# Attention scores from 96 stacked fp16 rows per head, brought through DRAM one iteration later

## The chip, the cores and the metric

The kernel runs on one core of one Trainium2 chip. The metric is the device time of one execution in microseconds. For scale, three executions of the kernel before took 1156.44, 1158.97 and 1160.72 us.

## What is computed

A Flamingo block: gated cross-attention over a short context, then a gated mixture of experts. There are 2 x 2048 tokens of width 512, 128 context rows, 16 heads of 32, 8 experts of which each token takes 2, and one shared expert.

```python
q = (layernorm(x) @ Wq.T + bq)       # 16 heads of 32
k, v = ctx @ Wk.T + bk, ctx @ Wv.T + bv
att = q @ k.T / sqrt(32)             # per head, [2048, 128]; two masks set entries to -1e9
x = x + tanh(g_xattn) * (softmax(att) @ v)
n = layernorm(x)
p = softmax(n @ router)              # the two largest of 8 weight the experts
x = x + tanh(g_ffn) * (sum of 2 experts(n) + shared expert(n))
```

## The kernel before

The tokens are 32 tiles of 128 rows. There are three passes. **Pass 1** does the attention, the second layernorm and the routing for one tile after the other, and cuts the experts' weights in two fp16 halves beside it. **Pass 2** runs 71 slots of 128 gathered rows through the experts. **Pass 3** does the shared expert and the output. The change is in pass 1; passes 2 and 3 only get other semaphore counts.

Pass 1 is a software pipeline written out by hand. Iteration `it` of every engine's `body` works on several tiles at once: a block that begins with `tile(J, v, lag)` works on tile `it - lag`. Iterations 0 to 11 are written out (`HEAD1`), 12 to 31 are a loop whose trip is two iterations (v = 0 and v = 1), and those from 32 to 39 drain the pipeline (`LAG1` = 8). The order within one iteration is the order of the code on each engine; between engines there are semaphores only. The lags before: 0 first layernorm's statistics; 1 normalised x (ScalarE L584); 2 its transposes (TensorE, L1046), its high fp16 half (ScalarE L556) and low half (VectorE L812), the query product (L1134 to L1136, 48 matmuls) and the move of q to SBUF (ScalarE L607, four instructions); 3 scores (L1099), masked scores with their row maxima (VectorE L782, 16 heads), the shift by the maxima (GpSimd L469) and the exponentials (ScalarE L570, L600); 4 transposes of the probabilities (L1046), their copy (ScalarE L563) and the product with the values (L1119); 5 to 8 the residual, second layernorm (L808 normalises), router and row lists.

The scores of four heads are one fp32 product: 128 rows of q, which hold four heads of 32, against `kbd`, in which each head's keys stand in its own 32 rows and 128 columns and zeros elsewhere.

```python
t.matmul(bank[2 + k % 2][:, :], q_t[u][:, k * P:(k + 1) * P], kbd[:, u, k, :],
         start=True, stop=True).then_inc(s_done, 1)
```

Beside the tiles' work, VectorE searches the weights' peaks in iterations 3 to 11 (L885, two chunks in each of 3 to 7, then one), iteration 11 ends with the spreading of these peaks over the partitions (`spread_peaks`, `scale_of`), and each trip of the loop cuts one chunk: ScalarE writes the high half behind v = 0 (L637), VectorE the low half behind v = 1 (L915). Iterations 32 to 34 cut three more (ScalarE L630, VectorE L907). SyncE issues the tile's loads and stores from one queue, in the order of its `body`.

## Time and profile before

| | us |
|---|---|
| three executions, median | 1158.97 (1156.44 to 1160.72) |
| the profiled execution | 1153.63, of which the span 1151.9 |
| pass 1, to the last cast of its row list | 523 |
| plan and first gathers, until TensorE is in full work | to about 560 |
| passes 2 and 3 | from there to 1152 |
| mean granted TensorE clock | 0.957 of 2.4 GHz |

Two executions of one kernel differ by up to 4 us here. The timelines count from the first instruction. A busy time counts overlapping instructions of an engine once; a matmul's own duration (0.22 us for one of 128 columns) includes its way through the array, so that what one adds to the engine's time is the distance between starts.

### The profile page before, as it was taken

Reading aid. Unit: us, or ns where it says so; the run is one execution under the profiler, and the core shown is the slowest. Engines: PE = TensorE matmul, PEld = TensorE weight load, DVE = VectorE, ACT = ScalarE, POOL = GpSimd, SP = SyncE. Lnnn points to the kernel's source line nnn. Section 1 sums busy time; section 2 is a strip of 40 time slices with the busy share of each in tenths; the row PEclk is TensorE's granted clock in tenths of the full one; section 3 lists DMA queues with packets and bytes.
Section 4 is the critical chain, followed back from the end, with each engine's and each line's share of the span. In section 5 each row is a group of like instructions: output and inputs, shape, how many; then the busy total and the mean of one; then the engine's idle time right before and its main releaser. Section 6 shows DMA issues by size and latency. Waiting matters only on the chain.

```text
span 1151.9 us, 26618 instructions
## 1 busy us (share of the span) xinstructions
PE 1044.5 (91%) x7344; PEld 670.6 (58%) x7345; DVE 823.4 (71%) x2938; ACT 530.7 (46%) x1041; POOL 444.0 (39%) x654
## 2 busy tenths in 40 slices
PE   5899969999999999851899999999999999999996
PEld 4677758777777777640455555555554444444443
DVE  5999868888888888673576666666665566666666
ACT  2455536666666666540444444444443223232322
POOL 4345547666666666442211221221110423232322
PEclk9999989999999999865899999999999999999999
DMA  7564753334433332432233333333332645454444
GB/s 284 184 237 168 165 118 95 95 95 93 109 80 108 104 91 90 101 93 73 83 111 118 109 119 118 109 118 119 109 119 71 184 148 166 152 169 150 168 150 128
DMA packets 76731, 146.96 MB, mean 128 GB/s; under 512 B 20912, under 2 KB 23088, under 8 KB 73872
## 3 DMA queue, kind: packets, MB, share of 16 engines
q1 hardware_dynamic: 46512, 66.01, 20.9%
q10 hardware_dynamic: 17280, 44.83, 10.3%
q0 software_dynamic: 12896, 35.58, 10.0%
q8 instruction: 22, 0.36, 0.2%
q14 instruction: 21, 0.17, 0.2%
HBM read 94.04 MB, written 52.35 MB: 127 GB/s over the span
## 4 chain that ended last, share of the span: by engine, by line
PE 58%; issue 11%; DVE 11%; POOL 8%; DMA 5%; ACT 3%; POOLq 1%; SPq 0%; another core or an unknown queue 0%; DVEq 0%; ACTq 0%
PE bank L1054 15%; PE bank L1055 15%; PE bank L1056 15%; PE bank L1046 8%; DVE arena L782 3%; PE bank L1099 3%; DMA arena<-in_x 3%; POOL arena L469 3%; PE bank L1119 2%; POOL token_of_row L505 2%; DVE arena L871 1%; DVE peak L885 1%; POOL arena L476 1%; ACT arena L607 1%; DMA token_of_row<-arena 1%
## 5 line engine op out<-in xcount | busy, mean ns | idle before, releaser
L1054 PE MATMUL bank<-weights,arena 128*128 (+1 forms) x682 | 260.0, 381 | 2.1 <-ACT arena L649 1.9
L1055 PE MATMUL bank<-weights,arena 128*128 (+1 forms) x682 | 260.0, 381 | 0.0
L1056 PE MATMUL bank<-weights,arena 128*128 (+1 forms) x682 | 259.7, 381 | 0.0
L1046 PE MATMUL bank<-ident,arena 128*128 128x128 f32 (+1 forms) x1592 | 188.3, 266 | 52.9 <-DMA arena<-normed_rows,arena 26.3
L1046 PEld LDWEIGHTS bank<-ident,arena 128*128 128x128 f32 (+1 forms) x1592 | 160.7, 132 | 99.9 <-issue 69.3
L516 POOL DMA_INDIRECT arena<-normed_rows,arena x71 | 67.1, 946 | 255.1 <-PE bank L1046 238.4
L1099 PE MATMUL bank<-arena 128*128 128x512 f32 x256 | 138.8, 646 | 11.0 <-DVE arena L782 8.9
L1119 PEld LDWEIGHTS bank<-arena 128*128 128x128 f32 x1024 | 128.3, 194 | 34.9 <-issue 28.0
L469 POOL TENSOR_TENSOR arena<-arena 128x512 f32<-128x512 f32 x96 | 101.3, 1055 | 83.0 <-DVE arena L782 81.9
L526 POOL DMA_INDIRECT arena<-expert_rows,arena x64 | 62.8, 982 | 173.8 <-DVE arena L1006 156.1
L1119 PE MATMUL bank<-arena 128*128 128x33 f32 x1024 | 125.3, 273 | 3.3 <-ACT arena L563 3.3
L782 DVE CUSTOM_DVE_ANT_0 arena<-bank,arena 128x128 f32<-128x128 f32 x512 | 116.8, 283 | 15.0 <-PE bank L1099 11.2
L570 ACT ACTIVATE arena<-arena 128x512 f32<-128x512 f32 x96 | 60.6, 631 | 125.5 <-POOL arena L469 125.2
L1056 PEld LDWEIGHTS bank<-weights,arena 128*128 128x128 f16 x682 | 66.9, 98 | 81.0 <-issue 1.3
L1054 PEld LDWEIGHTS bank<-weights,arena 128*128 128x128 f16 x682 | 66.9, 98 | 72.2 <-issue 4.4
L1055 PEld LDWEIGHTS bank<-weights,arena 128*128 128x128 f16 x682 | 66.8, 98 | 69.9 <-issue 1.1
L978 DVE TENSOR_SCALAR arena<-bank,arena,w_back 128x512 f32<-128x512 f32 x71 | 57.5, 810 | 55.5 <-PE bank L1056 55.4
L1134 PE MATMUL bank<-arena 128*128 128x128 f16 x512 | 87.4, 219 | 1.4 <-DVE arena L812 1.4
L1136 PE MATMUL bank<-arena 128*128 128x128 f16 x512 | 87.4, 219 | 0.0
L1135 PE MATMUL bank<-arena 128*128 128x128 f16 x512 | 87.4, 219 | 0.0
L505 POOL DMA_INDIRECT token_of_row<-arena x64 | 66.3, 1035 | 38.1 <-POOL arena L502 17.3
L658 ACT ACTIVATE arena<-arena 128x256 f16<-128x256 f32 x71 | 36.0, 508 | 91.3 <-DVE arena L990 91.3
(175 smaller groups left out, 1895.8 us busy)
## 6 DMA issues: line engine op xcount, KB each, us to landing
expert_rows<-arena ACTq DMA_DIRECT2D x71, 256.0 KB, 2.1
arena<-in_x SPq DMA_DIRECT2D x64, 256.0 KB, 2.8
weights<-in_w_gu ACTq DMA_DIRECT2D x8, 1024.0 KB, 4.9
x_rows<-arena SPq DMA_DIRECT2D x32, 256.0 KB
normed_rows<-arena SPq DMA_DIRECT2D x32, 256.0 KB
normed_transposed<-arena SPq DMA_DIRECT2D x32, 256.0 KB
arena<-normed_transposed SPq DMA_DIRECT2D x32, 256.0 KB, 3.2
arena<-x_rows SPq DMA_DIRECT2D x32, 256.0 KB, 3.5
```

What stands on the lines that cost most here:

```text
L469: g.tensor_tensor(sc, sc, mx, ALU.subtract).then_inc(shift_done, 1)
L505: g.indirect_dma_start(list_dram, bass.IndirectOffsetOnAxis(ap=row_i[u][:, k:k + 1], axis=0), tok_i[u], None).then_inc(rows_out[u], 16)
L782: last = d.tensor_tensor_reduce(score[u][:, hh * T:(hh + 1) * T], bank[2 + k % 2][:, h * T:(h + 1) * T], mask_bias[u], 1.0, LOWEST, ALU.ad ...
L1046: last = t.transpose(dst[:, c * P:(c + 1) * P], src[:, c * P:(c + 1) * P], (ident16 if src.dtype == F16 else ident)[:, :])
L1054: t.matmul(dst, hi[:, rows], w_hi(c), start=(c == 0), stop=False)
L1055: t.matmul(dst, hi[:, rows], w_lo(c), start=False, stop=False)
L1056: last = t.matmul(dst, lo[:, rows], w_hi(c), start=False, stop=(c == chunks - 1))
L1099: t.matmul(bank[2 + k % 2][:, :], q_t[u][:, k * P:(k + 1) * P], kbd[:, u, k, :], start=True, stop=True).then_inc(s_done, 1)
L1119: last = t.matmul(bank[6 + half][:, at:at + D + 1], probs_t[k % 2][:, h * P:(h + 1) * P], vaug[:, u, k * HG + h, :], start=True, stop=True)
L1134: t.matmul(dst, wq[:, 0, at:at + P], x_hi[:, xs], start=(ci == 0), stop=False)
L1135: t.matmul(dst, wq[:, 0, at:at + P], x_lo[:, xs], start=False, stop=False)
L1136: last = t.matmul(dst, wq[:, 1, at:at + P], x_hi[:, xs], start=False, stop=(ci == EC - 1))
```

## The change

- **Scores.** q and k are written as fp16 halves, high and low. For each head 96 rows are stacked by `stack`: part 0 (the high half), part 1 (the low half) and part 0 of its 32 rows, of q and of k alike. One fp16 matmul of 96 x 128 by 96 x 128 per head gives what four heads together had from one fp32 matmul of 512 columns: 16 matmuls for four.
- **The way of q.** ScalarE writes the high half of q (one instruction instead of four), VectorE the low half (new, first in its next iteration), SyncE stores both to DRAM (256 KB) and, when that has landed, loads the stack with three DMAs of 128 KB. Scores and all behind them are therefore one iteration later: lag 4 and so on, `LAG1` = 9, one iteration more in all.
- **The way of k**, once, in iteration 2: peak, scale, halves, a store to DRAM and three loads; the memset of `kbd` goes away and the sixteen small moves of k become four of all partitions.
- **Bias of q**: four more fp16 matmuls of 64 rows per tile, instead of the bias operand of L607. The exponentials scale by `score_scale`.
- **Order.** The transposes of x stand behind the first value product on TensorE. ScalarE's high half of x stands behind the first two probability copies and ahead of the exponentials. VectorE's low half of x stands behind the second group of maxima. SyncE issues q's store, x, the residual's x and the stack first, then the stores.
- **Semaphores** of passes 2 and 3 are merged; the spreading of the peaks uses bank 4 in place of bank 0.

```diff
+SMALL = 2.0 ** -20
+BIAS_PART = 32.0
+Q_DOWN = 2.0 ** -19
+STACK = 3 * D
...
+    q_dram = nc.dram_tensor("query_halves", [B, 2, P, E], F16).ap()
+    k_dram = nc.dram_tensor("key_halves", [2, P, EC * B * T], F16).ap()
...
-        kbd = carve(B * EC * HG * T).rearrange("p (b c n) -> p b c n", b=B, c=EC)
+        k_stack = carve(B * H * T // 2).bitcast(F16)
...
-        q_t = [carve(E) for _ in range(2)]
+        q_halves = carve(E).bitcast(F16)
+        q_stack = [carve(H * T // 2).bitcast(F16) for _ in range(2)]
...
-        LAG1, LAG2, LAG3, SPAN2 = 8, 4, 4, 4
+        LAG1, LAG2, LAG3, SPAN2 = 9, 4, 4, 4
...
-                n, j, u = tile(J, v, 6)
+                n, j, u = tile(J, v, 3)
+                if live(n, NT):
+                    hold(sp, sp_passed, (q_ready, n + 1))
+                    sp.dma_start(q_dram[u].rearrange("a p n -> p a n"), q_halves.rearrange("p (a n) -> p a n", a=2)).then_inc(q_out[u], 16)
+                n, j, u = tile(J, v, 0)
+                if live(n, NT):
+                    need(sp, xn_ready, n - 1)
+                    sp.dma_start(x_in[u], x_tiles[bass.ds(j + u * HALF, 1)].rearrange("a p d -> (a p) d")).then_inc(x_here[u], 16)
+                n, j, u = tile(J, v, 5)
+                if live(n, NT):
+                    need(sp, x1_ready, n - 1)
+                    sp.dma_start(x_res[u], x_tiles[bass.ds(j + u * HALF, 1)].rearrange("a p d -> (a p) d")).then_inc(res_here[u], 16)
+                n, j, u = tile(J, v, 3)
+                if live(n, NT):
+                    hold(sp, sp_passed, (q_out[u], 16 * (j + 1)))
+                    hold(sp, sp_passed, (s_done, group(n - 2, EC - 1)))
+                    stack(q_stack[u], q_dram[u], q_stacked[u])
+                n, j, u = tile(J, v, 7)
...
+                n, j, u = tile(J, v, 8)
...
-                n, j, u = tile(J, v, 0)
-                if live(n, NT):
-                    need(sp, xn_ready, n - 1)
-                    sp.dma_start(x_in[u], x_tiles[bass.ds(j + u * HALF, 1)].rearrange("a p d -> (a p) d")).then_inc(x_here[u], 16)
+                n, j, u = tile(J, v, 1)
+                if live(n, NT):
...
-                n, j, u = tile(J, v, 4)
-                if live(n, NT):
-                    need(sp, x1_ready, n - 1)
-                    sp.dma_start(x_res[u], x_tiles[bass.ds(j + u * HALF, 1)].rearrange("a p d -> (a p) d")).then_inc(res_here[u], 16)
+            def stack(dst, src, done):
+
+                for at, part in enumerate((0, 1, 0)):
+                    sp.dma_start(dst[at * D:(at + 1) * D, :].rearrange("d (h n) -> d h n", h=HG),
+                                 src[part].rearrange("(h d) n -> d h n", h=HG)).then_inc(done, 16)
 
+                if it == 2:
+                    sp.wait_ge(k_lo_set, 1)
+                    sp.dma_start(k_dram.rearrange("a p n -> p a n"), k_halves.rearrange("p (a n) -> p a n", a=2)).then_inc(k_out, 16)
+                    sp.wait_ge(k_out, 16)
+                    stack(k_stack, k_dram, k_stacked)
...
@@ ScalarE @@
             def body(J, v):
-                n, j, u = tile(J, v, 2)
-                if live(n, NT):
-                    act.wait_ge(xt_done, n + 1)
-                    need(act, q_done, n)
-                    a.activation(x_hi, bank[0][:, :], ACT.Copy, scale=X_SCALE).then_inc(hi_ready, 1)
-
                 def take_probs(k):
-                    n, j, u = tile(J, v, 4)
+                    n, j, u = tile(J, v, 5)
                     if live(n, NT):
...
                 take_probs(0)
                 take_probs(1)
+                n, j, u = tile(J, v, 2)
+                if live(n, NT):
+                    act.wait_ge(xt_done, n + 1)
+                    need(act, q_done, n)
+                    a.activation(x_hi, bank[0][:, :], ACT.Copy, scale=X_SCALE).then_inc(hi_ready, 1)
                 exponent(0)
...
-                        last = a.activation(sc, sc, ACT.Exp, bias=peaks_neg[:, h - H + HG:h - H + HG + 1])
+                        last = a.activation(sc, sc, ACT.Exp, scale=score_scale[:, :], bias=peaks_neg[:, h - H + HG:h - H + HG + 1])
...
                     act.wait_ge(q_done, n + 1)
-                    need(act, s_done, group(n - 2, EC - 1))
-                    for c in range(EC):
-                        last = a.activation(q_t[u][:, c * P:(c + 1) * P], bank[0][:, c * P:(c + 1) * P], ACT.Identity,
-                                            scale=w_back[:, 0:1], bias=bq_s[:, c:c + 1])
-                    last.then_inc(q_ready, 1)
+                    hold(act, act_passed, (q_out[(v - 3) % 2], 16 * (j + u)))
+                    a.activation(q_halves[:, 0:E], bank[0][:, :], ACT.Copy, scale=Q_DOWN).then_inc(q_hi_ready, 1)
 
             def beside(it):
+                if it == 2:
+                    act.wait_ge(scale_set, 3)
+                    a.activation(k_halves[:, 0:EC * B * T], k_full, ACT.Copy, scale=w_scale[:, 5:6]).then_inc(k_hi_set, 1)
...
@@ VectorE @@
-                dve.wait_ge(kv_set, 1)
+                dve.wait_ge(kv_mm, 1)
                 for c in range(EC):
-                    dve.wait_ge(kv_mm, 1)
-                    for h in range(HG):
-                        rows = slice(h * D, (h + 1) * D)
-                        last = d.tensor_scalar(kbd[rows, :, c, h * T:(h + 1) * T], bank[K_BANK + c][rows, 0:B * T].rearrange("p (b t) -> p b t", b=B),
-                                               bk_s[rows, c:c + 1], float(D) ** -0.5, ALU.add, ALU.mult)
-                last.then_inc(kv_set, 1)
+                    last = d.tensor_scalar(k_full[:, c * B * T:(c + 1) * B * T], bank[K_BANK + c][:, 0:B * T], bk_s[:, c:c + 1],
+                                           float(D) ** -0.5, ALU.add, ALU.mult)
+                link(last)
+                d.tensor_reduce(peak[:, 20:21], k_full, AX.X, ALU.max, apply_absolute_value=True).then_inc(peak_set, 1)
+                spread_peaks(1, 2)
+                scale_of(5, 1, 20, SMALL)
+                d.tensor_scalar(score_scale[:, :], w_back[:, 0:1], w_back[:, 5:6], 1.0 / Q_DOWN, ALU.mult, ALU.mult).then_inc(kv_set, 1)
+                dve.wait_ge(k_hi_set, 1)
+                d.scalar_tensor_tensor(k_halves[:, EC * B * T:], k_full, w_scale[:, 5:6], k_halves[:, 0:EC * B * T],
+                                       ALU.mult, ALU.subtract).then_inc(k_lo_set, 1)
...
+                n7, j7, u7 = tile(J, v, 8)
+                n8, j8, u8 = tile(J, v, 9)
+                n, j, u = tile(J, v, 3)
+                if live(n, NT):
+                    dve.wait_ge(q_hi_ready, n + 1)
+                    d.scalar_tensor_tensor(q_halves[:, E:2 * E], bank[0][:, :], Q_DOWN, q_halves[:, 0:E], ALU.mult, ALU.subtract).then_inc(q_ready, 1)
...
-                n, j, u = tile(J, v, 2)
-                if live(n, NT):
-                    dve.wait_ge(hi_ready, n + 1)
-                    d.scalar_tensor_tensor(x_lo, bank[0][:, :], X_SCALE, x_hi, ALU.mult, ALU.subtract).then_inc(lo_ready, 1)
...
                 maxima(1)
-                normalise(1, 5)
+                n, j, u = tile(J, v, 2)
+                if live(n, NT):
+                    dve.wait_ge(hi_ready, n + 1)
+                    d.scalar_tensor_tensor(x_lo, bank[0][:, :], X_SCALE, x_hi, ALU.mult, ALU.subtract).then_inc(lo_ready, 1)
...
@@ TensorE @@
-                    n, j, u = tile(J, v, 3)
+                    n, j, u = tile(J, v, 4)
                     if live(n, NT):
-                        pe.wait_ge(q_ready, n + 1)
+                        pe.wait_ge(q_stacked[u], 16 * PARTS * (j + 1))
+                        pe.wait_ge(k_stacked, 16 * PARTS)
                         need(pe, max_done, group(n, k - 2))
-                        if it_is_first(n, k):
-                            pe.wait_ge(kv_set, 2)
-                        t.matmul(bank[2 + k % 2][:, :], q_t[u][:, k * P:(k + 1) * P], kbd[:, u, k, :],
-                                 start=True, stop=True).then_inc(s_done, 1)
+                        for h in range(HG):
+                            q_at, k_at = (h * EC + k) * P, ((h * EC + k) * B + u) * T
+                            last = t.matmul(bank[2 + k % 2][:, h * T:(h + 1) * T], q_stack[u][0:STACK, q_at:q_at + P],
+                                            k_stack[0:STACK, k_at:k_at + T], start=True, stop=True)
+                        last.then_inc(s_done, 1)
...
-                                last = t.matmul(dst, wq[:, 1, at:at + P], x_hi[:, xs], start=False, stop=(ci == EC - 1))
+                                t.matmul(dst, wq[:, 1, at:at + P], x_hi[:, xs], start=False, stop=False)
+                            last = t.matmul(dst, bq_half[:, co * P:(co + 1) * P], bias_row[:, :], start=False, stop=True)
...
                 mix_values(0)
+                n, j, u = tile(J, v, 2)
+                if live(n, NT):
+                    pe.wait_ge(xn_ready, n + 1)
+                    need(pe, q_ready, n)
+                    transposes(bank[0], xn[u], EC).then_inc(xt_done, 1)
                 scores(2)
...
             def beside(it):
                 if it == 2:
+                    turn_peaks(1, 2)
                     values()
                 if it == SPREAD_IT:
-                    pe.wait_ge(q_ready, it - 1)
-                    turn_peaks(0, 2)
-                    pe.wait_ge(scale_set, 4)
+                    turn_peaks(4, 3)
+                    pe.wait_ge(scale_set, 5)
```

## Rows read from the trace of the kernel before

**Rows 1.** The page: busy time by engine, and two groups of instructions.
```profile
PE 1044.5 (91%) x7344; PEld 670.6 (58%) x7345; DVE 823.4 (71%) x2938; ACT 530.7 (46%) x1041; POOL 444.0 (39%) x654
...
L1119 PE MATMUL bank<-arena 128*128 128x33 f32 x1024 | 125.3, 273 | 3.3 <-ACT arena L563 3.3
L782 DVE CUSTOM_DVE_ANT_0 arena<-bank,arena 128x128 f32<-128x128 f32 x512 | 116.8, 283 | 15.0 <-PE bank L1099 11.2
```
**Rows 2.** Windows: stretch, length, busy PE, PEld, DVE, ACT, POOL, clock, DMA, GB/s.
```profile
60.00:120.00 60.00, 55.99 (x535) 46.76 (x535) 57.78 (x253) 37.21 (x84) 32.27 (x51) 1.00 0.55 186
...
300.00:360.00 60.00, 56.65 (x540) 47.34 (x536) 49.94 (x272) 39.73 (x89) 39.21 (x56) 0.94 0.32 92
```
**Rows 3.** Timeline of VectorE over two iterations: start, duration, instruction, idle time before.
```profile
317.53 0.54 DVE L808 TENSOR_SCALAR arena<-arena 128x512 f32<-128x512 f32 x1
320.85 0.69 DVE L812 SCALAR_TENSOR_TENSOR arena<-bank,arena 128x512 f16<-128x512 f32 x1 [2.78 <-ACT arena L556]
322.42 0.29 DVE L782 CUSTOM_DVE_ANT_0 arena<-bank,arena 128x128 f32<-128x128 f32 x1 [0.88 <-PE bank L1099]
...
346.24 0.54 DVE L808 TENSOR_SCALAR arena<-arena 128x512 f32<-128x512 f32 x1
```
**Rows 4.** Timeline of ScalarE between the same two iterations.
```profile
316.94 1.50 ACT L607 ACTIVATE arena<-bank,bq_s,w_back 128x128 f32<-128x128 f32 x4
318.30 2.02 ACT L637 ACTIVATE weights<-weights,w_scale  x1
320.20 0.62 ACT L556 ACTIVATE arena<-bank 128x512 f16<-128x512 f32 x1
```
**Rows 5.** Windows of TensorE alone around that place: stretch, length, busy, clock, DMA.
```profile
316.00:320.00 4.00, 2.49 (x32) 0.95 0.87 309
320.00:324.00 4.00, 4.00 (x14) 0.62 0.06 17
```
**Rows 6.** Timeline of VectorE: first and last start of twenty loop iterations, and the peaks.
```profile
155.16 0.69 DVE L871 BATCH_NORM_STATS2 arena<-arena 128x6 f32<-128x512 f32 x1 [4.73 <-DMA arena<-in_x]
...
163.28 0.55 DVE L808 TENSOR_SCALAR arena<-arena 128x512 f32<-128x512 f32 x1 [0.45 <-DVE w_scale L741]
...
448.74 0.54 DVE L808 TENSOR_SCALAR arena<-arena 128x512 f32<-128x512 f32 x1
```
**Rows 7.** The chain that ended last, in order of time: start, its length, what.
```profile
328.30 0.06 PE bank L1134
...
334.44 1.72 PE bank L1099 x4
```
**Rows 8.** Timeline of VectorE at the start.
```profile
26.28 7.91 DVE L762 TENSOR_SCALAR arena<-bank,bk_s 32x256 f32<-32x256 f32 x16
...
35.42 0.68 DVE L812 SCALAR_TENSOR_TENSOR arena<-bank,arena 128x512 f16<-128x512 f32 x1
...
41.65 4.45 DVE L885 TENSOR_REDUCE peak<-weights 128x1 f32<-128x2048 f32 x2
```
**Rows 9.** Timeline of TensorE at the start.
```profile
25.56 7.08 PE L1081 MATMUL bank<-arena 128*128 128x512 f32 x16
```
**Rows 10.** DMA issues before 180 us: x loads, count, KB, us to landing.
```profile
arena<-in_x SPq DMA_DIRECT2D x24, 256.0 KB, 7.3
```
**Rows 11.** The same from 180 to 450 us.
```profile
arena<-in_x SPq DMA_DIRECT2D x37, 256.0 KB, 2.7
```
**Rows 12.** The queue of SyncE: start and duration of one issue.
```profile
49.85 0.43 SPq L384 DMA_DIRECT2D arena<-in_x  x1
```
**Rows 13.** Timeline of VectorE in the iterations behind the loop.
```profile
463.36 2.35 DVE L907 SCALAR_TENSOR_TENSOR weights<-weights,w_scale 128x2048 f16<-128x2048 f32 x1 [3.55 <-ACT weights L630]
...
479.74 2.35 DVE L907 SCALAR_TENSOR_TENSOR weights<-weights,w_scale 128x2048 f16<-128x2048 f32 x1 [4.07 <-ACT weights L630]
482.01 0.54 DVE L808 TENSOR_SCALAR arena<-arena 128x512 f32<-128x512 f32 x1
...
495.27 2.35 DVE L907 SCALAR_TENSOR_TENSOR weights<-weights,w_scale 128x2048 f16<-128x2048 f32 x1 [2.16 <-ACT weights L630]
```

237 lines of the change are left out of this document (128 added, 109 removed).

## The prediction

> **What bounds the kernel now.** I read the page's busy times first: TensorE is at work for 91% of the span, VectorE for 71% [rows 1]. That is a mean over passes with different limits, so I went to the windows by stage. The change is in pass 1. There both engines are close to full: between 60 and 120 us VectorE has 57.78 of 60 us, in the loop (300 to 360 us) TensorE 56.65 and VectorE 49.94 [rows 2]. Work taken from TensorE is therefore worth no more than the room VectorE leaves.
>
> That room is read from VectorE's timeline over one trip of the loop, two iterations [rows 3]. From one L808 (317.53) to the next but one (346.24) are 28.71 us. In it VectorE waits twice for long: 2.78 us at L812 for ScalarE's high half of x, 0.88 us at L782 for the first scores. The rest, 28.71 - 2.78 - 0.88 = 25.05 us, is work, with short gaps of 0.2 us between dependent instructions. ScalarE's timeline shows where the 2.78 us come from [rows 4]: four moves of q (1.50 us) and the split of a weight chunk (L637, 2.02 us) stand ahead of L556 in its queue. TensorE is held by the same moves of q, since its transposes of x wait for the bank: in this window it is busy for 2.49 of 4 us, and in the next 4 us its granted clock is 0.62 of 2.4 GHz, thus a good part of it at 1.2 GHz [rows 5]. The mean over the loop: iterations 12 to 31 take 448.74 - 163.28 = 285.46 us [rows 6], 28.55 us a trip.
>
> **TensorE's part.** Two fp32 score products take 1.72 us of the chain, four 3.44; an fp16 matmul of 128 columns starts 0.06 us after the one before it [rows 7]. The new sixteen are 16 x 0.06 = 0.96 us, the four of the bias 0.24. TensorE loses 3.44 - 1.20 = 2.2 us of work in each of 32 iterations, 72 us in all. From 56.65 / 60 x 14.27 = 13.5 us an iteration it falls to 11.2, and no longer bounds. If it alone counted, the kernel would be 72 us faster; that is the far end on that side.
>
> **VectorE's part in the loop.** It gains one instruction per tile, the low half of q. Its form (fp16 from PSUM, 128 x 512, one fp16 operand) is L812's, 0.69 us [rows 3], 1.38 us a trip. The two long waits should go: the moves of q become one instruction (L556's form, 0.62 us in place of 1.50 [rows 4]), x's low half now stands behind two groups of maxima, and scores come from a tile that was ready an iteration ago. Work alone gives 25.05 + 1.38 = 26.4 us a trip. Some wait stays. In the v = 1 iteration ScalarE comes out of the chunk's split 2.02 us late, and then has two copies of probabilities ahead of x's high half, which in turn needs TensorE's first value product and the transposes. Starting from the low half of q at 0, ScalarE is free at about 1.4, has copied by 2.4, TensorE's value product and transposes end at 3.3 (125.3 / 1024 x 8 = 1.0 for eight products [rows 1] is in it), the high half at 4.0; VectorE reaches the low half at 3.5 (0.69 + 0.54, eight maxima at 116.8 / 512 = 0.23 [rows 1], 0.5 of small ones). So about 0.4 us. And TensorE now idles more in each trip, so more of its stretches will be at 1.2 GHz; one of them in front of that same path costs VectorE about 1 us. I take 0.5 us a trip for it. Sum 26.4 + 0.4 + 0.5 = 27.3, against 28.55: -1.25 us a trip, -12.5 us in ten. Bounds: 26.4 (-21.5) and 28.9 (+3.5, where TensorE is late at each step, see the second rival).
>
> GpSimd isn't next: it is busy for 39.21 of 60 us [rows 2], and gets no work in the loop. ScalarE loses 0.88 us an iteration and isn't next either.
>
> **SyncE's queue in the loop.** It issues ten DMAs an iteration in place of five or six, 0.43 us each [rows 12], 4.3 us of 13.7. It waits for the low half of q, stores it, issues two x loads while the store is under way, waits for the store, and issues three loads. By the x loads' 2.7 us to landing [rows 11] the stack is there 0.7 + 0.43 + 2.7 + 1.3 + 2.7 = 7.8 us after VectorE's iteration begins, and TensorE asks for it after a whole iteration, 13.7 us. The x load of the same iteration is issued at about 1.6 and needed near its end. The stores of the residual and of the normalised rows now stand behind the wait for the stack, with some 4 us to spare. I cost all this at nothing; if the cover were gone, each us of delay would be one us an iteration. The 640 KB of new traffic raises a DMA share of 0.32 [rows 2] by the ratio of bytes (five transfers of 256 KB before) to about 0.5: the engines are not full.
>
> The Trainium skill speaks of this way too. DMA: Bandwidth & Descriptors, section Anatomy of one DMA, gives each DMA a fixed cost of some 2 us that hardly depends on its size and comes mostly from confirming the write. By it the two dependent steps would cost 4 us beside their bytes, which is still hidden in the loop; the landing times of [rows 11] already hold it, and no run here shows the part alone.
>
> **The start.** The sixteen small moves of k (L762) take 7.91 us, 0.49 each; four of all partitions, at the same 0.49, end at 26.3 + 2.0 = 28.3 [rows 8]. Then come a search of 1024 columns (half of one of the two L885, 1.1), the spreading and one scale (3.6; with two scales it took some 4.4, what is left of the 8.1 us from 155.16 to 163.28 [rows 6] behind 1.4 of the iteration's rest and a search of 2.2), ScalarE's half (half of L637, 1.0) and VectorE's (half of L907's 2.35 [rows 13], 1.2): 35.2. The store and the loads follow, and only behind them SyncE's x of tile 3, which VectorE needs to end iteration 3. Two landings in a row, at 2.7 to 7.3 us each [rows 10, 11], and 1.7 us of issues: x is there at 42 to 51.5, I take 47.5. With 0.9 us of statistics and the two searches (4.45) iteration 4 begins at 52.8. TensorE's values product (7.08 us, [rows 9]) moves behind the peaks' spreading and ends at 39, under the same cover. Its first scores need the stack of tile 0, another two landings: +1.5, at 54.3. Before, the first scoring iteration began at 35.42 [rows 8]. So 18.9 us are lost, but iterations 3 to 11 scored nine tiles there and score eight now. Those nine took 163.28 - 35.42 = 127.9 us, of which 4.4 spreading and 4.7 a wait for x, so 13.2 each. The start costs 18.9 - 13.2 + 8 x 0.69 = +11.2; taken off are the waits for ScalarE and the first scores there (about 4.8) and one search and the lighter mix of what drops out (some 3). Rounded, +3.5 us at the loop's first iteration, with 0 and +10 as its ends, from the two landing times.
>
> **The end.** One iteration with scores more. Such a one, without the layernorm of x, took 495.27 - 2.16 - 482.01 = 11.1 us [rows 13], at a slow TensorE; with the short scores about 10.5. In the three before, VectorE waits for ScalarE's chunk (3.55, 4.07, 2.16 us [rows 13]). The shorter move of q takes 0.88 off two of them, faster scores about 1.6 over all, the low halves of q give 2.1 back: -1.3. The end costs +9, from +6 to +12. Pass 2 and 3: nothing, their waits are the same ones under other counts.
>
> **Sum.** +3.5 - 12.5 + 9 = 0. The profiled execution took 1153.63, so it would be again; it was 5.3 us under the median of the runs. I forecast the median: 1159 us.
>
> **The rivals.** *VectorE runs without waits.* For it: in the iterations between 60 and 120 us it is at 96% [rows 2] although TensorE is then nearly full too. Then the trip is 26.4, the start +1 and the end +9: -21.5 + 10 = -11.5, 1147 us. Faster. Chance 0.34.
>
> *TensorE's clock.* This ends on the other side. TensorE's work a trip falls to 22.4 us, of which the stretch at the low clock cost 0.38 x 4 = 1.5, so to 20.9 at 2.4 GHz, in 27: near a quarter of the time idle, in pieces of 1 to 2 us, where one piece of 1.5 us was enough for a stretch at 1.2 GHz [rows 5]. If half of its time is granted at 1.2 GHz, the work takes 20.9 / 0.75 = 27.9 us, longer than VectorE's 27.3, and two engines that hand over to each other several times a trip then take more than either: 28.9. That gives +3.5 in the loop, and with a slower start (+5) and end (+10) +18, 1177 us. It decides from about two low stretches a trip on, where there was one. Against it: TensorE waits for VectorE at most places, so much of a low stretch is cover. Chance 0.16. The Trainium skill has the rule, in TensorE: Matmul & The Clock Gate, section A second HAM failure mode: short idles between groups of matmuls are enough to let the clock swing. By [rows 5] the trace agrees for the one place there is.
>
> *The way through DRAM is late where the weights are loading.* There x loads take 7.3 us to land [rows 10]; the stack would need 0.7 + 0.43 + 7.3 + 1.3 + 7.3 = 17 us against iterations of 13.2. With 3 to 4 us of wait in half of eight iterations, +14, and the kernel is at 1172 us. It decides where a landing takes over 5.4 us. Against it: a chunk's load is over well before the next, so few stacks meet one. Chance 0.12.
>
> The forecast itself, within about 6 us of no change, has 0.38.
>
> **How the numbers follow.** 0.5% (6 us) is about what a measurement of this kernel can tell from no change. Faster 0.34 is the first rival, slower 0.28 the two others, 0.38 the forecast. The likeliest case alone covers 1153 to 1165. The range reaches to the first rival and 3 us beyond it, and to the late way through DRAM: 1144 to 1175.
>
> **What would show it.** L1099 at 16 matmuls an iteration, about 0.9 us. VectorE at over 90% of the loop with no wait of 2.8 us at x's low half; a trip of 27.3 us, the loop from about 167 to 440 us; the low half of q at 0.69. No wait of TensorE for the stack after 180 us. The pass 1 end at 523 give or take 6. The prediction is wrong if the trip is under 26.5 or over 28.5, if TensorE waits for the stack in the loop, or if the first scores come before 48 or after 60 us.

## The result and the profile after

The changed kernel takes 1190.32 us (median of 4 runs, 1176.83 to 1199.91) against 1157.70 us for the kernel before (4 runs). Two of the four runs, the profiled one of 1199.91 us among them, showed a lower granted clock and over 1.5% more time than the fastest, so the ratio is that of the other two, 1.0195 with a 95% interval of 1.0125 to 1.0265. In a second comparison it took 1181.35 us (6 runs) against 1154.45 (17 runs): ratio 1.0249, interval 1.0208 to 1.0291. It is 2.5% slower. The forecast was 1159 us and no change, and the range ended at 1175. Executions also scatter more than the 4 us of the first three: those 17 of the kernel before lie between 1149.46 and 1162.29 us, the six of the changed kernel between 1177.53 and 1191.09.

What follows reads the profile of the second comparison, an execution of 1180.61 us. Its page, busy times by engine and the group of the new score products:

```profile
PE 1047.2 (89%) x7731; PEld 708.2 (60%) x7732; DVE 839.3 (71%) x2970; ACT 528.5 (45%) x946; POOL 443.0 (38%) x658
...
L1155 PE MATMUL bank<-arena 96*128 96x128 f16 x512 | 52.4, 244 | 28.7 <-DMA arena<-query_halves 16.8
```

TensorE is as busy as before [rows 1] although its long products are gone, and it sat idle for 16.8 us ahead of the new ones, waiting for q's stack. Windows by stage, columns as in [rows 2]:

```profile
60.00:120.00 60.00, 54.66 (x552) 49.36 (x551) 55.84 (x198) 34.71 (x66) 25.64 (x44) 0.86 0.64 216
120.00:180.00 60.00, 41.26 (x427) 37.85 (x424) 42.20 (x211) 25.15 (x52) 26.29 (x41) 0.79 0.70 185
180.00:240.00 60.00, 56.19 (x532) 52.61 (x531) 45.84 (x252) 37.59 (x70) 33.16 (x48) 0.78 0.71 134
240.00:300.00 60.00, 55.39 (x548) 50.92 (x547) 51.07 (x264) 37.38 (x71) 38.28 (x56) 0.82 0.73 120
300.00:360.00 60.00, 54.77 (x600) 50.08 (x599) 54.23 (x266) 38.43 (x73) 40.51 (x58) 0.91 0.71 149
```

The kernel before, in two of these stretches:

```profile
180.00:240.00 60.00, 56.29 (x521) 45.67 (x519) 51.05 (x277) 39.61 (x88) 41.58 (x59) 0.97 0.32 90
240.00:300.00 60.00, 56.73 (x546) 47.78 (x546) 50.52 (x271) 40.40 (x88) 40.83 (x57) 0.97 0.41 97
```

Two columns differ. The granted clock between 180 and 300 us is 0.78 and 0.82, so a large part of that stretch ran at 1.2 GHz. The DMA share is 0.7, where it was 0.32 to 0.41 and where I had worked out "about 0.5".

To see where the time goes I take one mark in each iteration that no kernel here moves, the start of VectorE's statistics of x (L871 before, L935 after). For tiles 11 and 31, and the last low half of pass 1, VectorE's timeline after:

```profile
170.74 0.68 DVE L935 BATCH_NORM_STATS2 arena<-arena 128x6 f32<-128x512 f32 x1
...
464.70 0.68 DVE L935 BATCH_NORM_STATS2 arena<-arena 128x6 f32<-128x512 f32 x1
...
538.16 0.69 DVE L932 SCALAR_TENSOR_TENSOR arena<-bank,arena 128x512 f16<-128x512 f32 x1 [0.74 <-ACT arena L641]
```

Before, the mark of tile 11 is at 155.16 [rows 6] and the last low half at 511.5: pass 1 ends 26.7 us later, and the spans differ by 26.9 (1178.8 and 1151.9). Passes 2 and 3 cost what they did. The stages of one profiled execution of each kernel, in us between these marks ("way" is q's store to DRAM and the three loads of the stack):

| kernel | mark 3 | 3 to 9 | 9 to 11 | 11 to 21 | 21 to 31 | to the end of pass 1 |
|---|---|---|---|---|---|---|
| before | 40.8 | 80.3 | 34.0 | 146.7 | 143.1 | 66.6 |
| changed | 49.5 | 80.6 | 40.6 | 155.8 | 138.1 | 73.5 |
| changed, without the way | 50.5 | 76.8 | 26.4 | 147.9 | 136.1 | 73.5 |
| changed, way in the loop alone | 50.2 | 80.5 | 28.5 | 153.0 | 146.3 | 73.9 |
| changed, way unread, SyncE still waits | 49.4 | 81.6 | 42.9 | 157.5 | 138.0 | 79.1 |
| changed, reload at 32 | 49.9 | 80.0 | 29.2 | 156.4 | 137.8 | 85.1 |
| changed, reload spread | 49.7 | 88.4 | 29.3 | 158.2 | 142.5 | 73.9 |
| no way, scores four times | 50.2 | 83.7 | 30.3 | 166.9 | 145.1 | 81.1 |
| before, x moved | 40.5 | 82.2 | 31.3 | 148.8 | 137.7 | 66.1 |

Each row is one execution, and a stage scatters by several us. The kernel with the spread reload has the code of the changed kernel up to mark 9 and yet shows 88.4 for 80.6. The medians below decide. What is sharp is iteration 11. VectorE and TensorE in the changed kernel, waits between 140 and 182 us (total, times, longest):

```profile
PE bank L1155 <- DMA arena<-query_halves: 14.2, 1, 14.2
DVE arena L872 <- DMA normed_rows<-arena: 13.8, 1, 13.8
```

SyncE's queue shows why. L383 is q's store, L416 the stack, issued once the store has landed, L404 the store of the normalised rows. Iteration 11, then one late in the loop:

```profile
147.66 0.38 SPq L383 DMA_DIRECT2D query_halves<-arena  x1
148.08 0.51 SPq L387 DMA_DIRECT2D arena<-in_x  x1
148.64 0.47 SPq L391 DMA_DIRECT2D arena<-in_x  x1
162.64 1.27 SPq L416 DMA_DIRECT2D arena<-query_halves  x3
163.96 0.43 SPq L400 DMA_DIRECT2D x_rows<-arena  x1
164.43 0.43 SPq L404 DMA_DIRECT2D normed_rows<-arena  x1
...
427.12 0.38 SPq L383 DMA_DIRECT2D query_halves<-arena  x1
...
429.55 1.28 SPq L416 DMA_DIRECT2D arena<-query_halves  x3
```

Over pass 1 (40 to 540 us) TensorE waits 16.8 us for the stack, of which 0.3 after 180 us, and VectorE 19.1 us in three waits for the store of the normalised rows. Before there was no wait for that store.

From the store's issue to the stack's the forecast had 3.1 us (0.43 + 2.7). Late in the loop it is 2.4. In iteration 11 it is 15.0, in the one before 6.9, and twice in the first half of the loop 7.9 and 9.3. In iterations 10 and 11 ScalarE's queue is loading 3 MB of w_down again. The Trainium skill has a reason for so late a landing, in DMA: Bandwidth & Descriptors, section Queues, rings and completion order: the increment that reports a transfer lands only after every earlier write of the same DMA engine, from whichever queue. Nothing here shows that step by itself, but the trace does not speak against it.

### The profile page after: what moved, and what is told of

Read it like the earlier page. It is cut to its first block, busy times and chain, and to the rows that moved or that the text cites. A ratio compares the mean times of both kernels' runs of the same rounds, so it can differ in the third digit from the quotient of the medians.

```text
span 1198.1 us, 28092 instructions
## 1 busy us (share of the span) xinstructions
PE 1071.2 (89%) x7731; PEld 728.5 (61%) x7732; DVE 840.3 (70%) x2970; ACT 528.9 (44%) x946; POOL 442.0 (37%) x658
## 4 chain that ended last, share of the span: by engine, by line
PE 65%; DVE 12%; issue 9%; DMA 7%; POOL 3%; ACT 1%; SPq 1%; POOLq 1%; DVEq 0%; another core or an unknown queue 0%; ACTq 0%
PE bank L1111 14%; PE bank L1113 14%; PE bank L1112 14%; PE bank L1103 10%; PE bank L1176 6%; DVE arena L842 4%; PE bank L1155 2%; PE bank L1192 2%; DMA arena<-in_x 1%; DMA normed_rows<-arena 1%; PE bank L1194 1%; PE bank L1193 1%; DVE peak L949 1%; DMA token_of_row<-arena 1%; DVE arena L935 1%
## 5 line engine op out<-in xcount | busy, mean ns | idle before, releaser
L1103 PE MATMUL bank<-ident,arena 128*128 128x128 f32 (+1 forms) x1592 | 220.7, 288 | 52.5 <-DMA arena<-normed_rows,arena 27.2
L1103 PEld LDWEIGHTS bank<-ident,arena 128*128 128x128 f32 (+1 forms) x1592 | 181.9, 146 | 83.1 <-issue 49.6
L1176 PE MATMUL bank<-arena 128*128 128x33 f32 x1024 | 154.1, 305 | 3.8 <-ACT arena L606 2.1
L1176 PEld LDWEIGHTS bank<-arena 128*128 128x128 f32 x1024 | 146.3, 223 | 8.4 <-ACT arena L606 3.2
L842 DVE CUSTOM_DVE_ANT_0 arena<-bank,arena 128x128 f32<-128x128 f32 x512 | 116.7, 282 | 20.1 <-PE bank L1155 14.2
L1113 PEld LDWEIGHTS bank<-weights,arena 128*128 128x128 f16 x682 | 67.0, 98 | 81.1 <-issue 1.8
L1192 PE MATMUL bank<-arena 128*128 128x128 f16 x512 | 105.0, 237 | 3.1 <-DVE arena L889 3.1
L1193 PE MATMUL bank<-arena 128*128 128x128 f16 x512 | 103.9, 235 | 0.0
L1194 PE MATMUL bank<-arena 128*128 128x128 f16 x512 | 103.4, 234 | 0.4 <-issue 0.4
L613 ACT ACTIVATE arena<-arena,score_scale 128x512 f32<-128x512 f32 x96 | 69.0, 719 | 51.2 <-POOL arena L508 49.9
L606 ACT ACTIVATE arena<-bank 128x512 f32<-128x512 f32 x128 | 70.3, 589 | 45.5 <-PE bank L1103 45.2
L1155 PE MATMUL bank<-arena 96*128 96x128 f16 x512 | 54.9, 252 | 30.2 <-DMA arena<-query_halves 16.8
```

Source lines behind the costliest of these rows:

```text
L606: a.activation(probs_t[k % 2], bank[4 + k % 2][:, :], ACT.Copy).then_inc(pt_ready, 1)
L842: last = d.tensor_tensor_reduce(score[u][:, hh * T:(hh + 1) * T], bank[2 + k % 2][:, h * T:(h + 1) * T], mask_bias[u], 1.0, LOWEST, ALU.ad ...
L1103: last = t.transpose(dst[:, c * P:(c + 1) * P], src[:, c * P:(c + 1) * P], (ident16 if src.dtype == F16 else ident)[:, :])
L1113: last = t.matmul(dst, lo[:, rows], w_hi(c), start=False, stop=(c == chunks - 1))
L1155: last = t.matmul(bank[2 + k % 2][:, h * T:(h + 1) * T], q_stack[u][0:STACK, q_at:q_at + P], k_stack[0:STACK, k_at:k_at + T], start=True, ...
L1176: last = t.matmul(bank[6 + half][:, at:at + D + 1], probs_t[k % 2][:, h * P:(h + 1) * P], vaug[:, u, k * HG + h, :], start=True, stop=True)
```

## The experiments

Five theories. **A**: the stores, put behind the stack's wait in SyncE's queue, are late. **B**: q's way itself, by its traffic. **C**: TensorE with less to do runs at the lower clock, which eats what was saved. **S**: the reload of w_down in iterations 10 and 11 holds q's way up. **W**, against B taken as the bytes: the waits for q's way. All ratios are to the kernel before on the same chip, with their 95% intervals.

**The changed kernel again**, unchanged: the reference for the others.

> The changed kernel once more, unchanged: a second profile to read the others against. Expected by every theory: 1177 to 1192 us, ratio to before 1.015 to 1.025, and again one long wait of VectorE for the store of normed_rows in iteration 11 (14.2 us in the first profile), if that wait belongs to the order of the queue and isn't an accident of one execution (then it is gone, and the time is near 1177).

1181.35 us, 1.0249 (1.0208 to 1.0291). The long wait is there again (13.8 us): it belongs to the kernel.

**The stores ahead of the wait** (A).

```diff
+ (x1, xn2, x2t stores of tiles n-7, n-8)     # behind q's store
  (two loads of x)
  hold(q_out); hold(s_done); stack(...)
- (x1, xn2, x2t stores of tiles n-7, n-8)
```

> Changed kernel with SyncE's three stores (x1, xn2, x2t) issued ahead of the two waits for q's store and the stack, right behind q's own store. Theory A (the loss is what stands behind the stack's wait in SyncE's queue, above all the 14.2 us wait of iteration 11): VectorE no longer waits for normed_rows, 14 to 20 us less than the changed kernel, 1162 to 1172. Theory B (it is the 128 KB stores and 1 KB packets of q's way that slow every transfer): at most 3 to 5 us less. Theory C (TensorE's clock falls because it has less to do): no change, or up to 3 us less.

1181.41 us, 1.0236 (1.0199 to 1.0273): nothing. VectorE's wait for the rows is gone, but between 118 and 182 us TensorE waits 15.7 us for the stack and VectorE 7.6 for x. A falls as the explanation of the 24 us: which transfer is late depends on the order, that one is late doesn't. The two waits of SyncE, for the low half of q and for q's store, still stand in its queue here.

**Without q's way** (B).

```diff
-if live(n, NT):                # q's store, and the stack
+if isinstance(n, int) and 0 <= n < 2:
...
-pe.wait_ge(q_stacked[u], 16 * PARTS * (j + 1))
+pe.wait_ge(q_stacked[u], 16 * PARTS)
```

> Changed kernel in which q goes through DRAM for tiles 0 and 1 only; all later scores are taken from the stacks of those two, so the fresh q is left out and the DMA way (one store, three loads a tile) with it; all products and evictions stand. Theory A: the same gain as from stores first, 14 to 20 us less than the changed kernel. Theory B: 25 to 35 us less, 1150 to 1160, DMA share of the loop back to about 0.35 and packets of 2048 bytes back to about 114 ns. Theory C: no more than 5 us less, and the granted clock between 180 and 300 us stays at 0.80 or below (0.80 and 0.78 in the changed kernel; 0.88 later in its loop).

1157.53 us (12 runs), 1.0036 (1.0011 to 1.0062). B holds in that the way as a whole costs 1.0249 / 1.0036 = 1.021, some 24 us. Two things go with it at once, though: its traffic, and the two waits of SyncE ahead of x and of the stores. The DMA share does not fall to the 0.35 expected, and the clock of 180 to 300 us is still low in part:

```profile
180.00:240.00 60.00, 56.66 (x560) 51.36 (x560) 52.45 (x269) 37.42 (x71) 39.47 (x56) 0.83 0.51 90
240.00:300.00 60.00, 55.01 (x613) 49.50 (x613) 55.68 (x292) 40.44 (x78) 42.19 (x60) 0.94 0.44 92
```

**Each score product four times** (C), in the changed kernel and in the one without the way.

```diff
+for _ in range(4):
     last = t.matmul(bank[2 + k % 2][...], q_stack[u][...], k_stack[...], start=True, stop=True)
```

> Changed kernel with each of the 16 score products of a tile issued four times (same result each time): 48 more products of 0.107 us at most, 5.1 us a tile, so that TensorE has in a tile what it had before the change. Theory C: the granted clock rises to 0.90 or more in the loop and the time falls by 5 to 15 us or at least stays. Theories A and B, with TensorE on the path of the loop: 3 to 5 us a trip more where TensorE ends last, 30 to 60 us more in all; if TensorE had slack, 0 to 10 us more.

> The kernel without q's way (tiles 0 and 1 alone, fresh q left out) and with each score product issued four times: TensorE's work of a tile is again what it was before the change, 5.1 us more. Theory C2 (TensorE's shorter work is worth nothing, since the granted clock falls by as much: 0.83 to 0.94 in its loop against 1.00 with the moves of x alone, both 276 us from tile 10 to tile 30): 1152 to 1162, loop 274 to 282, clock 0.97 or more. Rival: TensorE's work counts in the trip: 30 to 50 us more, 1185 to 1200.

1191.00 us, 1.0296 (1.0245 to 1.0348) with the way; 1195.60, 1.0312 (1.0261 to 1.0362) without. The 5.1 us a tile in the expectation were too many. They came from the group's mean (54.9 / 512 = 0.107 us), which holds the way through the array once for every four products; 32 of them in a row take 1.95 us, 0.061 each, and the filler 2.9 us a tile. TensorE's timeline and a window of the kernel without the way, scores four times:

```profile
421.20 1.95 PE L1158 MATMUL bank<-arena 96*128 96x128 f16 x32
```
```profile
420.00:480.00 60.00, 59.15 (x796) 55.37 (x796) 53.61 (x262) 38.02 (x72) 40.80 (x57) 1.00 0.33 90
```

With work to fill its pauses TensorE has the full clock in this stretch, as C says, but it is busy for 59.15 of 60 us and the trip is 29.0 us (145.1 / 5). C's forecast of the time, no rise, fails in both kernels. Without the way the filler costs 1.0312 against 1.0036, some 32 us; with it 1.0296 against 1.0249, some 5 us, which the intervals do not tell from nothing. With the filler q's way costs nothing that shows (1.0296 against 1.0312): its price is one of a kernel whose TensorE has room. The lower clock by itself is not what made the kernel slower: without the way it is low too, and the time is within 0.4% of before. Whether the way also costs through the clock, which it lowers further (0.82 against 0.94 between 240 and 300 us), was not separated.

**The three moves of x alone, in the kernel before.**

```diff
 scores(1); mix_values(0)
+transposes(bank[0], xn[u], EC)        # TensorE, was first in the body
...
 take_probs(0); take_probs(1)
+a.activation(x_hi, ...)               # ScalarE, was ahead of them
...
 maxima(1)
+d.scalar_tensor_tensor(x_lo, ...)     # VectorE, was ahead of maxima(0)
```

> Kernel before, with the three moves of x alone: TensorE's transposes of x behind mix_values(0), ScalarE's x_hi ahead of its exponentials, VectorE's x_lo behind maxima(1); scores as before. By the prediction's sum for the moves (the waits of 2.78 and 0.88 us in a trip of 28.55 go, TensorE's work of a trip stays as it was): 26.9 to 28.0 us a trip, 5 to 15 us less than before, 1140 to 1150. Rival: TensorE with the long scores is the bound of the trip once VectorE doesn't wait (56.5 of 60 us busy), and nothing is gained, 1152 to 1158. Second rival: x_lo now comes later than the queries want it and TensorE waits there instead: 1160 or more.

1147.77 us, 0.9929 (0.9908 to 0.9950): 7 us faster, the only part of the change that was shown to pay. VectorE's timeline in the trip that [rows 3] showed before, all its waits over 0.5 us:

```profile
320.89 0.29 DVE L781 CUSTOM_DVE_ANT_0 arena<-bank,arena 128x128 f32<-128x128 f32 x1 [1.91 <-PE bank L1092]
324.00 0.69 DVE L824 SCALAR_TENSOR_TENSOR arena<-bank,arena 128x512 f16<-128x512 f32 x1 [0.62 <-ACT arena L572]
```

3.66 us of waits have become 2.53, and the trip is 27.5 us (137.7 / 5) where it was 28.6. The changed kernel without the way has one wait in the same trip and takes 27.2 us:

```profile
319.99 0.29 DVE L844 CUSTOM_DVE_ANT_0 arena<-bank,arena 128x128 f32<-128x128 f32 x1 [1.20 <-PE bank L1157]
```

So once x is moved, the rest of the change without the way (the short products, less VectorE's new low half of q) is worth 0.3 us a trip in these two executions, less than they scatter. Over the whole kernel it costs: 1.0036 against 0.9929.

In the first half of the loop neither kernel gains (148.8 and 147.9 against 146.7). The moves alone had a granted clock of 1.00 there between 180 and 240 us and 0.97 between 240 and 300, so in their case a low clock is not the reason.

**Where the way costs: parts of it.** First the way for tiles 0 to 8, then 0 to 6, then 0, 1 and 9 to 31 (the conditions of the second diff, with these bounds).

> Changed kernel in which q goes through DRAM for tiles 0 to 8 only (the iterations that are written out); in the loop all scores are taken from the stacks of tiles 7 and 8, so fresh q is left out there. From the traces of the changed kernel (second run) and of the kernel without q's way: iteration 12 starts at 178.5 against 161.6 us, and the next 20 iterations take 290.0 against 279.9. Theory S (most of the way's price falls in iterations 10 and 11, where q's store and loads share the queues with 7 MB of w_down): 6 to 12 us less than the changed kernel, 1169 to 1175. Theory L (the price is paid evenly, by the DMA share of 0.7 in the loop): 17 to 24 us less, 1157 to 1164.

> Changed kernel in which q goes through DRAM for tiles 0 to 6 only, so in the iterations 3 to 9; from iteration 10 on all scores are taken from the stacks of tiles 5 and 6 and fresh q is left out. The kernel with the way for tiles 0 to 8 took 1182.7 us, the one with tiles 0 and 1 alone 1157.5. Theory T (the price is paid in iterations 10 and 11, where it stood next to 3 MB of w_down and the bursts of slow packets): 1155 to 1162, iteration 12 within 3 us of the kernel without the way. Rival (an even price of every iteration in the written-out part): 1170 to 1178, as 5 of the 7 tiles that cost are still there.

> Changed kernel in which q goes through DRAM for tiles 0, 1 and 9 to 31, not for 2 to 8; the scores of those seven take old stacks, fresh q is left out there. Theory F (in the loop the way is hidden; the 24 us are all paid in the written-out iterations): 1155 to 1163. Theory G (the loop's first half pays some 8 us, in the bursts of slow packets): 1163 to 1172. Rival: every part costs about the same whatever the others do: 1170 or more.

1182.71 us, 1.0224 (1.0194 to 1.0253); 1176.60, 1.0162 (1.0111 to 1.0212); 1172.51, 1.0122 (1.0075 to 1.0170). Less 0.0036 each: 1.9% for tiles 0 to 8, 1.3% for 0 to 6, 0.9% for the loop alone, 2.1% for all. The theory that iterations 10 and 11 hold all of it (T) falls: the even price is nearer. The way up to tile 8 costs more than either theory of its expectation allowed. The loop pays too: 1172.51 us lies half a us above G and within the rival, by which each part costs the same whatever the others do. The start alone and the loop alone make 2.7% together, where all of it costs 2.1%, but the intervals of the ratios are 0.3 to 0.5% wide on each side, so a sum is not ruled out.

**The reload of w_down** (S). One of three chunks at iteration 32, then all three, then twelve pieces of 256 KB at iterations 10, 11 and one a trip; this last also in the kernel before. (The first moved one chunk of three, not five of seven as its expectation says, so little could be seen of it.)

```diff
-if it == CHUNKS:
+if it == NT:                                   # in short: all three
     for i in range(CHUNKS, ALL_CHUNKS - 1): act.dma_start(raw(i), chunk_src(i))
```
```diff
+def reload_piece(k):
+    act.dma_start(weights[:, bass.ds(k * 512 + (CHUNKS + 1) * CH, 512)], w_down_flat[:, bass.ds(k * 512, 512)])
```

> Changed kernel with five of the seven w_down chunks of 1 MB reloaded at iteration 32 in place of iteration 10. Theory S: TensorE's wait for the stack in iteration 11 (14.2 us) falls below 4 us, iteration 12 starts at 163 to 168 and the time is 10 to 15 us less, 1166 to 1171, less some 2 to 6 us that ScalarE then waits for the first late chunk behind the loop. Theory L: at most 5 us less. Third way: the reload was only one of several loads in those iterations (DMA share 0.70 there with q's way, 0.64 without), and the wait stays above 8 us.

> Changed kernel with all three chunks of w_down (1 MB each) that are loaded again at iteration 10 loaded at iteration 32 instead. (The kernel called reload late moved one of these three, not five of seven as its expectation said, and nothing came of it.) If the reload is what holds q's store in iterations 10 and 11: the wait for the stack in iteration 11 (14.2 us) falls below 4 us, the transposes' evictions of tile 10 start 10 to 14 us sooner; ScalarE then waits some 5 to 8 us for the first chunk behind the loop, so 1170 to 1177. Rival: the bursts of slow packets come without the reload as well: wait still above 6 us, and 1185 to 1192 with the late chunk.

> Changed kernel with the 3 MB reload of w_down in twelve pieces of 256 KB: one each at iterations 10 and 11 and one a trip in the loop. With the whole reload moved to iteration 32, iterations 10 and 11 took 29.2 us in place of 40.6 (ends of iteration 9 to 11), and the part behind the loop 85.1 in place of 73.5. If the reload holds q's way: 30 to 33 us for the two iterations, 73 to 75 behind the loop, 1168 to 1174. Rival: the pieces disturb the loop as much as the block did the start, 1178 to 1186.

> Kernel before with the same spread reload. It has no stack to wait for, but one wait of 4.7 us for x in iteration 11; its iterations 10 and 11 took 34.0 us. If the reload matters without q's way too: 3 to 5 us less, 1150 to 1153. Rival: within 0.2% of before; then it is only q's two landings in a row that the reload hurts.

1189.35 us, 1.0313 (1.0284 to 1.0341); 1185.85, 1.0267 (1.0216 to 1.0318); 1185.99, 1.0260 (1.0213 to 1.0307); for the kernel before 1155.55, 0.9979 (0.9952 to 1.0006). With all three chunks gone from there, iterations 10 and 11 take 29.2 us in place of 40.6 and TensorE waits 0.2 us for the stack: S is right for that wait. The store still needs 8.3 and 7.6 us to the stack's issue there, in place of 6.9 and 15.0, so landings are slow without the reload as well. But behind the loop ScalarE then waits for the first chunk,

```profile
474.29 2.00 ACT L678 ACTIVATE weights<-weights,w_scale 128x2048 f16<-128x2048 f32 x1 [6.01 <-DMA weights<-in_w_down]
```

and that part takes 85.1 us in place of 73.5. Spread out, nothing is paid there (73.9), the two iterations still take 29.3, and yet the median doesn't move. S explains the most visible wait and not the time. That the spread pieces cost elsewhere what they save here is possible; one execution can't show it.

**A shorter way**: twelve copies from SBUF to SBUF (384 KB a tile in place of 640), without DRAM; then the same with x loaded first.

```diff
-sp.dma_start(q_dram[u]..., q_halves...)
+for at, part in enumerate((0, 1, 0)):
+    for h in range(HG):
+        sp.dma_start(q_stack[u][at * D:(at + 1) * D, h * E:(h + 1) * E], q_halves[h * D:(h + 1) * D, part * E:(part + 1) * E])
```

> Changed kernel with q's stack filled straight from q_halves in SBUF: twelve copies of 32 partitions x 1 KB a tile (384 KB) in place of one store of 256 KB and three loads of 128 KB through DRAM; SyncE issues 8 instructions more a tile. Theory B (traffic and two landings in a row): about half of the way's 24 us comes back, 1165 to 1173, and the wait for the stack in iteration 11 at least halves. Rival: what slows is the 1 KB pieces, of which there are as many as before in the loads: 1175 to 1183, no change. Rival 2: the longer issue at SyncE (12 x 0.43 us) makes x late and it is slower, 1185 or more.

> The kernel with twelve copies from SBUF to SBUF in place of q's way, and SyncE issues the two loads of x ahead of q's wait and copies. The direct kernel took 1244.8 us; its SyncE spent 6.6 to 7.5 us a tile on the twelve copies, and VectorE waited 22 us for x between 60 and 160 us. Theory X (the late x is what made it slow): the waits for x go, 30 to 50 us less, 1195 to 1215. Rival: the copies themselves land late, so that ScalarE waits for q_halves and TensorE for the stack: less than 15 us better, 1230 or more.

1244.78 us, 1.0788 (1.0761 to 1.0815), then 1191.15, 1.0306 (1.0262 to 1.0350). Rival 2 holds. SyncE's queue in the first, and VectorE's wait between 60 and 160 us:

```profile
112.24 7.49 SPq L386 DMA_DIRECT2D arena<-arena  x12
119.77 0.58 SPq L391 DMA_DIRECT2D arena<-in_x  x1
```
```profile
DVE arena L934 <- DMA arena<-in_x: 22.3, 6, 6.2
```

With x first 54 us come back, but not more: a shorter way in twelve pieces is no better than the one through DRAM. It moves fewer bytes (384 KB against 640) and costs no less (1.0306 against 1.0249), so the bytes by themselves do not set the price.

**Traffic or waits** (B against W). The same store and loads at the same places of SyncE's queue, from a constant tile into a buffer nobody reads; then with the stores first as well. TensorE and ScalarE no longer wait for the way, the first two tiles aside. SyncE does: its waits for the low half of q and for q's store stay, and one for the stack before is added.

```diff
+hold(sp, sp_passed, (q_stacked[1], 16 * PARTS * (n - 1)))    # SyncE waits for the stack before
-sp.dma_start(q_dram[u]..., q_halves...)
+sp.dma_start(q_dram[u]..., wq[:, 0, 0:2 * E]...)
...
 hold(q_out); ...                                # kept: SyncE waits for the store
-stack(q_stack[u], q_dram[u], q_stacked[u])
+stack(q_stack[1], q_dram[u], q_stacked[1])      # TensorE reads q_stack[0] for all tiles
```

> Changed kernel in which the same store and three loads are issued for every tile at the same places of SyncE's queue, but from a constant tile and into a buffer nobody reads; all scores are taken from the stack of tile 0, so fresh q is left out from tile 1 on. TensorE and ScalarE wait for none of it. Theory W (the waits are the price): 1157 to 1164, as without the way. Theory X (the traffic is, it delays x, the stores and the instructions of the other engines): 1172 to 1182. Between: the stores of the normalised rows, still behind SyncE's wait, hold VectorE in iteration 11 (13.8 us in the changed kernel): 1164 to 1172.

> The kernel before this one with SyncE's three stores ahead of the wait for q's store as well. If what was left there came from the stores behind the wait: 1157 to 1162. If it came from the traffic: as there, 1172 to 1182.

1185.53 us, 1.0247 (1.0211 to 1.0283), and 1195.45, 1.0333 (1.0306 to 1.0360). From tile 2 on TensorE and ScalarE wait for nothing of q's way, and the first kernel takes as long as the changed one; the second takes 10 us more. So the waits of these two engines are not the price, and that part of W falls. Other transfers are late instead. In the first kernel, waits between 118 and 182 us, then in the second:

```profile
DVE arena L878 <- DMA normed_rows<-arena: 16.4, 1, 16.4
```
```profile
DVE arena L941 <- DMA arena<-in_x: 12.5, 2, 7.3
```

But this is no kernel in which nobody waits. In the first one SyncE itself stands for 13.7 us in front of the next store, until the stack loaded before it has landed, and x and the stores of the next iteration stand behind it. SyncE's waits between 118 and 182 us, and its queue:

```profile
SPq L294 <- DMA arena<-query_halves: 14.1, 2, 13.7
```
```profile
142.85 4.09 SPq L420 DMA_DIRECT2D arena<-query_halves  x3
...
148.37 0.44 SPq L410 DMA_DIRECT2D normed_transposed<-arena  x1
162.59 0.38 SPq L387 DMA_DIRECT2D query_halves<-arena  x1
163.01 0.47 SPq L391 DMA_DIRECT2D arena<-in_x  x1
```

What VectorE waits for over pass 1 (40 to 540 us) is what stands behind SyncE's waits: in the first kernel 22.1 us for the stored rows, in the second, where the stores go first and x behind them, 33.0 us for x in thirteen waits. A kernel with the traffic and without SyncE's waits, or the reverse, was not run. What the way costs as traffic and what as waits in a queue that issues in order stays open.

SyncE's DMA queue between 200 and 460 us (packets, MB, share of 16 engines), before, without the way, and with the unread way:

```profile
q1 hardware_dynamic: 14445, 24.68, 33.5%
```
```profile
q1 hardware_dynamic: 14700, 25.07, 43.5%
```
```profile
q1 hardware_dynamic: 26843, 35.90, 72.0%
```

The bytes grow by 1.45, the packets by 1.86 and the engines' busy share by 2.1. From these lines one packet takes 0.096, 0.123 and 0.112 us (an estimate: share x 16 x 260 us over the packets), so most of the larger share goes with the number of packets. The x loads of this stretch do not land later for it: their median from issue to landing is 2.6 us before, 5.5 without the way and 2.8 in the changed kernel.

**The best version**: x moved and the reload spread, in the kernel before.

> Kernel before with the three moves of x (7 us less by themselves) and the spread reload. If the two add up: 1142 to 1146, 0.988 to 0.991 of before. Rival: the spread reload gives nothing once x's pieces are moved (iterations 10 and 11 took 31.3 us there already): 1147 to 1150.

1147.64 us, 0.9917 (0.9887 to 0.9948). The time is the rival's, but with 0.9929 for the moves alone and 0.9979 for the reload alone the intervals hold both a sum and no further gain. No gain of the spread reload is shown. Either kernel beats both the one before and the changed one, and the simpler one is enough.

## Why the prediction was wrong

The prediction's parts, against the changed kernel (in brackets: without the way).

- **What failed: SyncE's queue and q's way, "I cost all this at nothing".** It costs some 24 us (1.0249 against 1.0036); without it the time is 3 us above that of before, inside the forecast. The forecast took every landing at an undisturbed 2.7 us, found the stack in time and the stores "with some 4 us to spare", and took the traffic for free since "the engines are not full". The stack is mostly in time, as reckoned: 0.3 us of wait after 180 us. The 4 us to spare were not there at all times: the stack was issued 6.9 to 15.0 us after q's store in four iterations, and VectorE waited 19.1 us for the stores behind it. Taking single waits away, by another order, a later reload or an unread stack, does not bring the 24 us back. How they divide between the traffic and SyncE's own waits is open.
- **The loop, -12.5 us.** Between marks 11 and 31 it is +4.2 (-5.7). The forecast trip of 27.3 us came true, but in the second half alone: 27.6 (27.2). (The bound of 26.4 came from one trip of 28.71 us and was set against the mean of 28.55, 1.6 us too much in ten.) Over all ten trips the average is 29.4 us, beyond the 28.5 that was to be the sign of being wrong. In the first half the way adds 7.9 us, and even without it nothing is gained there (147.9 against 146.7). The clock of 0.78 to 0.83 between 180 and 240 us stands beside it, but the moves of x alone gain nothing there at a clock of 1.00 either.
- **The start, +3.5.** At mark 11 it is +15.6, beyond its upper end of +10 (-1.4). Without the way it was even better than forecast. The first scores came at 52.4 (53.3), forecast 54.3.
- **The end, +9.** +6.9 with and without the way, inside its bounds.
- **TensorE's work, 0.96 us for sixteen products.** The group's busy time is 52.4 us, 1.64 a tile or 0.102 each. That is no contradiction: the products come in groups of four or eight, and each group's busy time holds the way through the array once. Four take 0.39 us in a stretch with a granted clock of 1.00 and 0.61 us in one of 0.50 (1.2 GHz):

```profile
68.84 0.39 PE L1155 MATMUL bank<-arena 96*128 96x128 f16 x4
...
82.61 0.61 PE L1155 MATMUL bank<-arena 96*128 96x128 f16 x4
```

  Of 66 groups of four, 24 took longer than 0.46 us. A tile of one group of eight (0.61) and two of four is 1.39 us at the full clock, so the low clock accounts for about 0.25 of the 1.64.
- **VectorE's part.** Its direction was right: the two waits of 3.66 us a trip shrank to 1.2 without the way, in the trip shown. But the moves of x do nearly all of that alone (27.5 us a trip against 27.2), so the sum had credited the whole change with what three moved instructions bring. They alone make the kernel 7 us faster; in the one profile pass 1 is 5.0 us shorter, with 3.4 in the loop and 2.7 in iterations 10 and 11 gained and 1.9 lost in 3 to 9.
- **The rivals.** The late way where the weights load (0.12, 1172 us, by its own sum 1173) named the right place and mechanism: in iteration 11 the store lands late and TensorE waits. That its 14 us equal the 14.2 measured is luck, since they were 3 to 4 us in four iterations and became one wait. Nor is it the whole account, because with that wait gone the time stays. The clock (0.16, 1177 us) came near in time and is seen in the windows, but the kernel without the way has a low clock too and is only 0.4% slower than before. VectorE without waits (0.34) was reached in no run: no trip average came down to 26.4.

What stays open: how much of the price is traffic and how much is waiting in SyncE's queue, why taking away single waits, or the reload, doesn't bring it back, and why it vanishes when TensorE is full. Which transfer is late shifts with each edit. The way issued from another engine's queue was not tried, nor were larger pieces (the stack's rows are 1 KB).

## What to carry to other kernels

A transfer that mostly comes in time is not free: ask what its bytes do to the others, above all where weights are being loaded, and what stands behind its wait in the queue that issues it. A test for the bytes alone must take away the issuing engine's waits too, not only those of the engines that compute. When one change holds a reordering and a new algorithm, time the reordering alone; here it was the whole gain. The mean busy time of short products in small groups holds the way through the array, so price them by the distance between starts.

## What was not expected of the hardware

- The busy share of the DMA engines grew faster than the bytes: 24.68 to 35.90 MB in 260 us, 33.5% to 72.0%, while the packets went from 14445 to 26843. Without the way it was 43.5% at nearly the bytes and packets of before, so a share is no measure of bytes. Some packets are slow: over 1 us each between 60 and 560 us took 279 before, 505 without the way and 607 in the changed kernel, where a packet of 2 KB has a median of 84 ns. Their cause is open.
- A 256 KB store's way to the next issue took 2.4 us late in the loop, 15.0 us beside 3 MB of another queue's loads, and 7.6 us at the same place without them.
- Twelve copies of 32 KB keep SyncE's queue for 7.49 us, 0.62 each, where an issue took 0.43 [rows 12].
